# Second and third attention of a vision tower on one core: the six chunks of a group's projection stand in pairs, other operations ordered around them

## What is computed

```
h = tokenizer(x)
h = h + attn_0(layernorm(h))     # 12 heads of 16
h = h + ffn_0(layernorm(h))      # "C": q, k, v = x @ qkv_w + qkv_b, 12 heads of 64
h = h + attn_1(layernorm(h))     # "D": q, k, v = x @ w_qkv.T,       12 heads of 64
h = h + ffn_1(layernorm(h))      # masked MLP of width 3072
```

## Time and profile before

| | us |
|---|---|
| median of 3 runs (1360.43 to 1363.68) | 1361.9 |
| the profiled execution, its own time | 1363.47 |
| its span in the trace | 1361.2 |

### The profile page before, as it was taken

One profiled execution on the slowest core, in us unless ns is written; L12 is line 12 of the kernel. 1 busy time (PEld: TensorE's weight loads), 2 busy tenths in 40 slices (PEclk: granted clock), 3 DMA queues, 4 the chain that ended last, 5 costly groups with the idle time before them and its releaser, 6 DMA issues.

```text
span 1361.2 us, 25095 instructions
## 1 busy us (share of the span) xinstructions
PE 1183.3 (87%) x8302; PEld 1043.3 (77%) x8302; DVE 956.3 (70%) x2350; ACT 880.7 (65%) x3172; POOL 436.9 (32%) x467
## 2 busy tenths in 40 slices
PE   6988879868999999998699999999830089999998
PEld 4986657647888888897589989899710079999998
DVE  4669988865888898896478888888758833333333
ACT  1757788854999999987498998998731022222232
POOL 0000130204323333320343443443224035555555
PEclk8999999896999999999899999999965589999999
DMA  9202011000000000000000000000031000000000
GB/s 371 109 1 72 1 47 25 1 1 0 2 1 2 1 1 2 1 2 1 12 1 1 1 1 2 1 1 1 1 93 70 0 1 1 11 10 11 1 11 13
DMA packets 7849, 30.27 MB, mean 22 GB/s; under 512 B 2094, under 2 KB 4894, under 8 KB 6174
## 3 DMA queue, kind: packets, MB, share of 16 engines
q1 hardware_dynamic: 7724, 28.69, 6.2%
HBM read 26.92 MB, written 1.77 MB: 21 GB/s over the span
## 4 chain that ended last, share of the span: by engine, by line
PE 61%; DVE 9%; ACT 6%; issue 1%; POOL 1%; POOLq 0%; ACTq 0%; DVEq 0%
PE bank L1466 6%; PE bank L1431 6%; DVE f_eq L1750 4%; PE bank L1395 4%; PE bank L1457 4%; PE bank L1440 3%; PE bank L1415 3%; PE bank L1399 3%; PE bank L1396 3%; PE bank L1397 3%; PE bank L1398 3%; ACT t_p L1211 2%; PE bank L1814 2%; PE bank L1829 2%; PE bank L1816 2%; PE bank L1815 2%
## 5 line engine op out<-in xcount | busy, mean ns | idle before, releaser
L1211 ACT ACTIVATE t_p<-bank,t_nmax 108x108 f32<-108x108 f32 x792 | 267.2, 354 | 40.2 <-DVE t_nmax L740 39.4
L1935 POOL TENSOR_TENSOR f_hid_lo<-f_hid,f_hid_hi 128x432 fp32r<-128x432 f32 (+2 forms) x144 | 145.8, 1013 | 160.6 <-ACT f_hid_hi L1921 160.6
L1891 DVE SCALAR_TENSOR_TENSOR f_hid<-bank,f_maskT 128x432 f32<-128x432 f32 (+2 forms) x144 | 80.3, 558 | 165.6 <-PE bank L1818 164.4
L1047 POOL TENSOR_TENSOR t_sq<-t_raw 108x768 f32<-108x768 f32 x88 | 140.9, 1602 | 168.7 <-ACT t_raw L1151 167.7
L1921 ACT CAST f_hid_hi<-f_hid 128x432 fp32r<-128x432 f32 (+2 forms) x144 | 73.9, 513 | 181.1 <-DVE f_hid L1891 181.1
L1431 PE MATMUL bank<-t_kS,t_qT 128*108 128x216 f32 (+1 forms) x660 | 179.1, 386 | 3.3 <-DVE h L331 2.5
L1211 ACT ACTIVATION_READ_ACCUMULATOR t_p<-bank,t_nmax 108x1 f32 x792 | 166.1, 210 | 0.0
L758 DVE TENSOR_TENSOR t_p<-t_p,t_rinv 108x432 f32<-108x432 f32 x198 | 160.4, 810 | 6.8
L740 DVE TENSOR_REDUCE t_nmax<-bank 108x4 f32<-108x432 f32 x198 | 119.5, 603 | 59.2 <-PE bank L1431 58.8
L1440 PEld LDWEIGHTS bank<-ident,t_p 108*108 108x108 f32 x792 | 86.7, 132 | 54.7 <-ACT t_pT L1219 35.1
L1440 PE MATMUL bank<-ident,t_p 108*108 108x108 f32 x792 | 107.4, 258 | 22.2 <-ACT t_pT L1219 21.0
(11 more groups left out here) (227 smaller groups left out, 3250.6 us busy)
## 6 DMA issues: line engine op xcount, KB each, us to landing
A_x<-in_x SPq DMA_DIRECT2D x5, 1728.0 KB, 18.6
A_w<-in_tok_w SPq DMA_DIRECT2D x5, 768.0 KB, 7.2
f_raw_down<-in_w_proj SPq DMA_DIRECT2D x1, 2304.0 KB, 8.4
out_tokens<-h SPq DMA_DIRECT2D x21, 81.0 KB
f_raw<-in_w_mfc SPq DMA_DIRECT2D x1, 1536.0 KB, 7.3
f_raw<-in_w_mfc SPq DMA_DIRECT2D x2, 768.0 KB, 12.2
W_raw<-in_wC SPq DMA_DIRECT2D x1, 1159.0 KB
W_raw<-in_wC SPq DMA_DIRECT2D x2, 579.5 KB
```

Of the source, the lines that this page charges most:

```text
L1047: pool.tensor_tensor(sq, v, v, ALU.mult).then_inc(s["sq"], 1)
L1211: act.activation(b.p[g % 2][:, m, :], self.sbank[(3 * g + c) % 2][0:GT, n * GT:(n + 1) * GT], ACT.Exp, bias=b.nmax[:, m:m + 1], accum_out= ...
L1935: pool.tensor_tensor(self.hid_lo[m % 4][:, c], self.hid[m % 4][:, c], self.hid_hi[m % 4][:, c].bitcast(F32), ALU.subtract).then_inc(s["lo" ...
```

## The change

In the loops of "C" and "D", chunk 1 now stands directly behind chunk 0, chunk 3 behind chunk 2, and chunk 5 behind chunk 4, in TensorE's list. In ScalarE's list the copy of chunk 3 stands directly behind that of chunk 2, and the copy of chunk 5 directly behind that of chunk 4. Everything else keeps its order. `len(self.pv_split) - 1` is 1 in both kinds, so the call of `values` that is written anew is the same.

```
 # scalar
             if chunks:
                 copy_chunk(g + 2, 2)
+            if chunks:
+                copy_chunk(g + 2, 3)
             if before:
                 copy_o(g - 1, 0)
-            if chunks:
-                copy_chunk(g + 2, 3)
             if more:
                 copy_qk(g + 1, 1)
...
             if chunks:
                 copy_chunk(g + 2, 4)
+            if chunks:
+                copy_chunk(g + 2, 5)
             if kind == "C" and more:
                 copy_qk(g + 1, 2)
-            if chunks:
-                copy_chunk(g + 2, 5)
             if kind == "C" and more:
                 copy_qk(g + 1, 3)
 # tensor
             if chunks:
                 project(g + 2, 0)
+                project(g + 2, 1)
             if before:
                 turn_p(g - 1, 0)
             if this:
                 scores(g, 0)
             if before:
                 turn_p(g - 1, 1)
-            if chunks:
-                project(g + 2, 1)
             if more:
                 turn_qk(g + 1, 0)
...
             if chunks:
                 project(g + 2, 2)
+                project(g + 2, 3)
             if before:
                 values(g - 1, 0)
-            if chunks:
-                project(g + 2, 3)
             if more:
                 turn_qk(g + 1, 1)
             if this:
                 scores(g, 2)
             if before:
-                values(g - 1, len(self.pv_split) - 1)
+                values(g - 1, 1)
             if chunks:
                 project(g + 2, 4)
+                project(g + 2, 5)
             if more:
                 turn_qk(g + 1, 2)
-            if chunks:
-                project(g + 2, 5)
             if before:
                 output(g - 1)
```

## The result

The changed kernel takes 1391.6 us (median of 4 runs, 1387.6 to 1392.3) against 1362.0 for the kernel before in the same measurement: ratio 1.0211, 95% interval 1.0188 to 1.0234. That is 29.7 us slower. The span of the profiled execution grew by 27.8 us, from 1361.2 to 1389.0.

The account below looks back on a forecast made before the run. Loops through several engines, not TensorE's 99% busy list, were taken to set the 14.44 us period. 16.3 + 13.5 = 29.8 us on 1363.5 gave 1393.3 profiled; with the median 1.6 lower, 1392 us, range 1374 to 1402.

Parts of the forecast that it names:

- Part (1): Second attention, ScalarE-TensorE loop: chunk 1 behind chunk 0 delays the transposes of p and scores, +0.87 us per iteration.
- second longest loop: Third attention, through the second transposes of p and ScalarE's exponentials: 14.0 us, 14.9 with chunk 1, staying under 15.3.
- Part (2): Second attention: ScalarE's copy of chunk 5 delays the copy of q and so the x transposes, +0.38 us.
- The sum of 15.37: Second attention's loop after the change: 14.12 + 0.87 + 0.38 = 15.37 us, 0.93 over 14.44.
- Part (3): Third attention: chunk 5 delays the third q/k transposes and VectorE's q, +0.87 us per iteration, nothing absorbs it.
- Part (4): Both attentions: chunk 3 ahead of the values, its copy ahead of the output's, chunks 1, 3, 5 earlier: zero.
- The sum: Second attention 16.3 us (first hand-over about 0.3, 16 full ones at 0.93), third 13.5, in all 29.8.
- The clock: TensorE's waits grow to about 1 us per iteration, no loss taken; rival: clock falls, 1490 us, 3 in 100.
- TensorE's list as the bound: Rival: TensorE's amount of work sets the time in both attentions, no change, 1360 to 1364 us; 1 in 10.
- A saving of 0.08 us by a pair: Rival: each of three chunks saves 0.08 us of a start behind another operation, 1352 us; 7 in 100.
- Both attentions paid: Against the rival that only one stage pays: third alone 1375 us, second alone 1378; 15 in 100.
- wait for a late copy: Rival: chunks 3 or 4 also wait for late copies, 0.3 us more per iteration, 1404 us; 5 in 100.

Follow-up runs that it names:

- b_chunk1: Kernel before with only chunk 1 moved directly behind chunk 0 on TensorE: 1382.0 us, ratio 1.0139.
- a_copy5_back: Changed kernel with ScalarE's copy of chunk 5 back behind the first copy of q: 1382.2 us, ratio 1.0138 to the kernel before.
- b_copy5: Kernel before with only ScalarE's copy of chunk 5 moved ahead of the first copy of q: 1365.7 us, ratio 1.0020.
- a_chunk1_back: Changed kernel with chunk 1 back behind the second transposes of p on TensorE: 1370.0 us, ratio 1.0045 to the kernel before.
- a_chunk5_back: Changed kernel with chunk 5 back behind the third q/k transposes on TensorE, its copy staying ahead: 1386.3 us, ratio 1.0169 to the kernel before.
- a_chunk3_back: Changed kernel with chunk 3 back behind the first values and its copy behind that of the first output part: 1390.6 us, ratio 1.0202 to the kernel before.
- b_sum_later: Kernel before with VectorE's sum of the second half of a group's squares one iteration later, behind the first row maximum: 1354.4 us, ratio 0.9939.
- bs_chunk3_again: Repeat, with trace, of b_sum_later plus chunk 3 and its copy directly behind chunk 2 and its copy: 1354.1 us, ratio 0.9926 to the kernel before.
- b_chunk5_bias: b_chunk5 with GpSimd's bias addition moved ahead of its second squares: 1369.2 us, ratio 1.0044 to the kernel before.
- b_chunk5: Kernel before with only chunk 5 moved ahead of the third q/k transposes on TensorE: 1372.5 us, ratio 1.0069.

## Why the prediction was right, and where not

The forecast was 1392 us, and 1391.6 was measured.

*Part (1), chunk 1 in the second attention's loop, +0.87.* Right. The second chunk took 0.88, and b_chunk1 gave 15.02 where 14.12 + 0.87 = 14.99 had been summed. For the third attention the prediction had it in the second longest loop and so at no cost; there it was wrong, see part (3).

*Part (2), the copy of chunk 5, +0.38.* Right: 0.40 by a_copy5_back, with a slack of 0.30 by b_copy5. The sum of 15.37 measured 15.41.

*Part (3), chunk 5 in the third attention, +0.87 with "nothing absorbs it".* This step failed in size. The third attention grew by 0.50 per iteration, not 0.87. The runs show two reasons. VectorE's list is not of fixed length: shifted against GpSimd, line 785 took 0.69 us instead of 1.06 and the stretch 5.66 instead of 6.16, so this loop came to 14.79 (a_chunk1_back). And the loop that the prediction put second, through the second transposes of p, with its 14.9, became the longest: 14.93. b_chunk1 gives it by chunk 1 alone, a_chunk5_back keeps it without chunk 5. So the third attention's loss in the changed kernel is chunk 1's as well. The term was forecast as 13.5 us and measured 9.8 from iteration 0 to 20.

*Part (4), chunk 3: zero.* Nothing was lost by it, but the term was not zero: with its copy back behind that of the output the third attention went at 15.17 in its last eleven iterations (a_chunk3_back). Its copy's place bears on GpSimd's timing and so on line 785, and it is this part that brought VectorE's loop from 15.17 to 14.79.

*The sum.* Second attention 16.3 forecast, 1.9 + 15.5 = 17.4 measured; its first hand-over alone was mis-sized, 1.9 instead of 0.3, and the next one rose by 0.1 instead of 0.93. Third 13.5 and 9.8. The rest, +0.6, was counted as nothing. On the span these make 27.8 where 29.8 had been summed, and the medians moved by 29.7. So the nearness of 1392 to 1391.6 is in part luck: an error of -3.7 us in the third attention against +1.1 in the second and +0.6 in the rest, and 1.9 us between spans and medians.

*The clock.* Waits of 0.3 to 0.4 us, and no fall: 1.00 in both windows. TensorE's shown waits stayed under the 1 us forecast. In the second attention a part lies ahead of chunk 4, which waits for the copy of chunk 2; in the third it is 0.44 at 821.20:

```profile
513.03 0.42 PE L1395 MATMUL bank<-wC_hi,t_xh 128*108 128x384 f32 x1 [0.29 <-ACT t_raw L1151]
```

*The rivals.* TensorE's list as the bound is refuted by b_sum_later, which is faster with that list unchanged: 14.44 was a loop. A saving of 0.08 us by a pair is refuted, for chunk 3, by bs_chunk3_again. Both attentions paid. Chunk 4 does wait for a late copy, but in the second attention the period stayed within 0.04 us of the summed loop, so the wait adds no more than that.

## What to carry to other kernels

An engine that is busy 99% of the time need not set the period: compare the distance of two iterations with what the same list takes where its neighbours have less to do. Then write down each loop of engines with its sum, and also the second and third longest. An order that costs nothing in one engine's list can lengthen the loop that closes through it, and what a move adds is its duration less the slack of that loop. When a loop is cut, or grows, the next one can be close: here it was 0.14 us shorter (14.93 and 14.79), 0.24 (14.44 and 14.20) and 0.30 (the slack in b_copy5). And durations beside another engine's work can change as the phases shift.

## What was not expected of the hardware

VectorE's two subtract-and-scale operations on 108 partitions (line 785) took 0.59 to 0.61 us together where nothing ran beside them on GpSimd (as at 982.40 in the trace of before), 0.69 in most of the changed kernel, 0.80 beside line 1074 of GpSimd in b_chunk5_bias, and 1.06 to 1.09 in the middle of the third attention before, where GpSimd's squares and the bias addition ran beside them. In b_chunk5 both 0.69 and 1.04 to 1.08 occur, and the iteration time goes with them (14.81 and 15.16), though GpSimd's operations start at the same distances from line 785 to within 0.03 us; in the four short ones of 13 it is line 1071 of GpSimd that takes longer, 0.54 us instead of 0.41 to 0.44. What decides between the two is not shown. The start of a chunk behind transposes is dearer in looks only: in the timeline of before, its first matmul holds TensorE for 0.25 us instead of 0.17, but the four transposes ahead of it hold it for 0.31 instead of the 0.37 that they hold it ahead of the scores. So setting two chunks together moved the period by 0.02 us only.
